# Expert layer with stationary gate and up weights, packed weight transfers, a gather that skips empty rows, and down products of two tiles at a time

## What is computed

```python
x = hidden_states.reshape(-1, 512)                 # 448 tokens
probs = softmax(x @ router_w.T)                    # 32 experts
rw, sel = top_k(probs, 8); rw = rw / sum(rw)
for e in range(32):                                # w_gate, w_up: 512 x 192; w_down: 192 x 512
    w_e = sum(where(sel == e, rw, 0))
    h = silu(x @ wg[e]) * (x @ wu[e])
    acc += (h @ wd[e]) * w_e[:, None]
```

## Time and profile before

| | |
|---|---|
| median of 3 runs | 379.27 us (377.68 to 379.84) |
| profiled execution, its own time | 377.78 us |
| its span, first to last instruction | 375.9 us |
| busy: PE, DVE, ACT, POOL | 84%, 42%, 36%, 42% |
| expert loop, first `gate_up` to the last `down` | 136.5 to 358.5 us |
| moved by DMA | 88.6 MB |

### The profile page before, as it was taken

The page is one execution under the profiler, slowest core; times in us unless marked ns, Lnnn a source line. Parts: engine busy times, 40 slices in busy tenths (PEclk is TensorE's granted clock), DMA queues, the critical chain, the costliest instruction groups (busy, mean ns, idle before and its releaser), DMA issues.

```text
span 375.9 us, 4754 instructions
## 1 busy us (share of the span) xinstructions
PE 313.9 (84%) x1131; PEld 173.2 (46%) x1131; DVE 156.2 (42%) x465; ACT 137.0 (36%) x226; POOL 156.1 (42%) x144
## 2 busy tenths in 40 slices
PE   5799734558869469999999999999999999999910
PEld 1345211235536235555555555555555555555500
DVE  3348798174687833323322332332233233222102
ACT  3245738984873302222322322232232223223200
POOL 5304438643351122454355345435534543553230
PEclk9999976589989559999999999999999999999985
DMA  8599920097048331669999999999999999999667
GB/s 301 205 361 414 373 72 1 0 265 237 3 130 292 117 89 30 112 123 296 311 311 322 329 316 312 323 302 295 305 309 298 300 293 308 293 295 313 128 117 231
DMA packets 31310, 88.63 MB, mean 236 GB/s; under 512 B 4497, under 2 KB 4625, under 8 KB 30529
## 3 DMA queue, kind: packets, MB, share of 16 engines
q1 hardware_dynamic: 21936, 66.38, 51.7%
q0 software_dynamic: 8960, 21.63, 27.3%
q10 hardware_dynamic: 402, 0.48, 0.4%
HBM read 73.46 MB, written 15.02 MB: 235 GB/s over the span
## 4 chain that ended last, share of the span: by engine, by line
PE 66%; DVE 16%; ACT 5%; DMA 5%; issue 4%; POOL 2%; SPq 0%; DVEq 0%; POOLq 0%; ACTq 0%
PE ps L1025 30%; PE ps L1046 18%; PE ps L1035 5%; PE ps L1015 3%; DVE stats L1098 2%; PE ps L1054 2%; PE ps L901 2%; PE ps L851 2%; PE ps L927 2%; DMA sum<-w_t,add_idx 2%; ACT w_t L682 2%; DVE raw L1199 1%; POOL root_out L528 1%; DVE big L1193 1%; DVE amax L1246 1%
## 5 line engine op out<-in xcount | busy, mean ns | idle before, releaser
L599 POOL DMA_INDIRECT big<-token_rows,idx x40 | 39.6, 990 | 116.1 <-DVE idx L1338 98.0
L612 POOL DMA_INDIRECT sum<-w_t,add_idx x40 | 63.1, 1577 | 23.2 <-issue 13.0
L1388 DVE SCALAR_TENSOR_TENSOR w_t<-ps,big,w_t 128x192 f32<-128x192 f32 x40 | 16.7, 417 | 126.6 <-ACT w_t L812 126.6
L812 ACT ACTIVATE w_t<-ps 128x192 f32<-128x192 f32 x40 | 13.2, 331 | 109.9 <-PE ps L1025 109.9
L1025 PE MATMUL ps<-raw,w_t 128*128 128x384 f32 x144 | 51.1, 498 | 0.4 <-issue 0.4
L1025 PE MATMUL ps<-big,w_t 128*128 128x384 f32 x144 | 51.2, 499 | 0.0
L806 ACT ACTIVATE w_t<-ps 128x512 f32<-128x512 f32 x40 | 23.9, 597 | 47.6 <-PE ps L1046 47.6
L528 POOL TENSOR_TENSOR root_out<-root_in,minus_half 112x1 f32<-112x1 f32 x20 | 12.8, 640 | 59.1 <-DVE root_in L1111 59.0
L901 PE MATMUL ps<-w_t,q_t 128*112 128x512 bf16 (+1 forms) x96 | 26.1, 431 | 9.9 <-DVE h L1149 5.9
L1025 PEld LDWEIGHTS ps<-raw,w_t 128*128 128x128 f32 x144 | 25.9, 189 | 18.1 <-issue 3.8
L1025 PEld LDWEIGHTS ps<-big,w_t 128*128 128x128 f32 x144 | 25.9, 189 | 17.9 <-issue 3.6
(11 more groups left out here) (162 smaller groups left out, 397.7 us busy)
## 6 DMA issues: line engine op xcount, KB each, us to landing
big<-in_ffn_w_gate SPq DMA_DIRECT2D x18, 384.0 KB, 5.9
big<-in_ffn_w_up SPq DMA_DIRECT2D x18, 384.0 KB, 9.1
raw<-in_ffn_w_gate SPq DMA_DIRECT2D x18, 384.0 KB, 5.8
raw<-in_ffn_w_up SPq DMA_DIRECT2D x18, 384.0 KB, 7.1
raw<-in_ffn_w_down SPq DMA_DIRECT2D x18, 384.0 KB, 6.8
ring<-in_ffn_w_down SPq DMA_DIRECT2D x13, 384.0 KB, 7.2
big<-in_ffn_w_down SPq DMA_DIRECT2D x9, 384.0 KB, 7.5
big<-in_mlp_w_in SPq DMA_DIRECT2D x2, 1536.0 KB, 10.7
```

The lines of the kernel that those rows point to most:

```text
L599: nc.gpsimd.indirect_dma_start(got[:, s, :], None, rows_dram[:, :], bass.IndirectOffsetOnAxis(ap=idx[:, s:s + 1], axis=0)).then_inc(ld_got ...
L612: nc.gpsimd.indirect_dma_start(acc_dram[n][:, :], bass.IndirectOffsetOnAxis(ap=add_idx[:, s:s + 1], axis=0), y[:, s, :], None, compute_op= ...
```

## The change

- **Stationary weights.** `gate_up` holds blocks of 128 weight columns stationary and moves the 128 slots of x. Its output is h already transposed: gate and up of the first 128 hidden values, and one block in which gate and up of the last 64 stand together. 3 blocks x 4 inputs = 12 matmuls. `transpose_h` and its copy are gone. The gate value now enters as a scale in `y_out`.
- **Packed transfers.** The host lays each expert's gate, up and 128 rows of down into one array (`we_main`, 8 KB per row) and the other 64 rows of down into a second (`we_rest`). Two DMAs per expert instead of three. Eight slots, in four pairs; the two tiles of a pair keep their 64 rows in different halves of the 128 partitions. The unroll is U = 8.
- **Down of two tiles.** On even steps PE does `down` of t-2 and t-1: two matmuls with 128 rows, then two with 64 rows, the first in one row half, the second in the other.
- ACT's `y_out` and POOL's scatters of two tiles follow on odd steps.
- **Skipping gather.** Empty slots get an index beyond `token_rows`, and the gather leaves them out.

```diff
@@ gate_up @@
-                wg = gate_up_of(slot_of(st, 0))
+                wg = slots[st.u][:, 0:WG].rearrange("p (c o) -> p c o", c=DC)
                 pe.wait_ge(xt_ready, st.upto(0))
-                pe.wait_ge(ld_gu[st.u], st.landed(0, 32))
+                pe.wait_ge(ld_we[st.u], st.landed(0, 32))
                 wait(pe, hid_ready, st.upto(-2))
-                dst = bank(st.slot(0, 2))[:, 0:2 * IE].rearrange("p (n i) -> p n i", n=2)
-                for c in range(4):
-                    last = nc.tensor.matmul(dst, x_t[:, st.slot(0, 2), c, :], wg[:, :, c, :], start=c == 0, stop=c == 3)
+                for o in range(0, 3 * P, P):
+                    for c in range(DC):
+                        last = nc.tensor.matmul(bank(st.slot(0, 2))[:, o:o + P], wg[:, c, o:o + P], x_t[:, st.slot(0, 2), c, :],
+                                                start=c == 0, stop=c == DC - 1)
                 last.then_inc(gu_done, 1)
@@ down and transpose_h become down_two @@
-                for c in range(2):
-                    last = nc.tensor.matmul(bank(4 + st.slot(d, 2)), h_t[:, st.slot(d, 2), c, :], wd[:, c, :],
-                                            start=c == 0, stop=c == 1)
-                last.then_inc(y_done, 1)
-
-            def transpose_h(st):
...
+                wait(pe, y_ready, st.upto(d - 1))
+                for n in (d, d + 1):
+                    pe.wait_ge(hid_ready, st.upto(n))
+                    nc.tensor.matmul(bank(4 + st.slot(n, 2)), h_t[:, st.slot(n, HS), 0, :], slots[(st.u + n) % U][:, WG:WCOLS],
+                                     start=True, stop=False)
+                for n in (d, d + 1):
+                    nc.tensor.matmul(bank(4 + st.slot(n, 2)), h_t[rest_rows(st, n), st.slot(n, HS), 1, :],
+                                     slot_rest[(st.u + n) % U], start=False, stop=True).then_inc(y_done, 1)
@@ PE's loop @@
                 place_row(st, 3)
                 gate_up(st)
                 transpose_x(st, 1)
-                down(st, -1)
-                transpose_h(st)
-            down(Step(st.k, U - 1), 0)
+                if st.u % 2 == 0:
+                    down_two(st, -2)
+            down_two(Step(st.k, U - 2), 0)
@@ ACT's loop @@
             for st in steps_from(act, more_i, more_ready):
+                if st.u % 2:
+                    y_out(st, -3)
+                    y_out(st, -2)
                 act.wait_ge(gu_done, st.upto(0))
                 wait(act, hid_ready, st.upto(-1))
-                nc.scalar.activation(sg[:, :], bank(st.slot(0, 2))[:, 0:IE], ACT.Silu).then_inc(silu_ready, 1)
+                nc.scalar.activation(sg[:, 0, :], bank(st.slot(0, 2))[:, 0:P], ACT.Silu)
+                nc.scalar.activation(sg[IB:P, 1, :], bank(st.slot(0, 2))[0:IB, 2 * P:3 * P], ACT.Silu).then_inc(silu_ready, 1)
                 x_turned(st, 1)
-                y_out(st, -1)
@@ DVE's loop @@
+                dve.wait_ge(ld_got[s], st.gathered(0))
+                wait(dve, y_ready, st.upto(-4))
+                nc.vector.tensor_copy(gate_w[:, s:s + 1], gate)
                 dve.wait_ge(silu_ready, st.upto(0))
-                dve.wait_ge(ld_got[s], st.landed(0))
-                wait(dve, ht_done, st.upto(-2))
-                nc.vector.scalar_tensor_tensor(hid[:, st.slot(0, 2), :], bank(st.slot(0, 2))[:, IE:2 * IE], gate, sg[:, :],
-                                               ALU.mult, ALU.mult).then_inc(hid_ready, 1)
+                wait(dve, y_done, st.upto(-HS))
+                nc.vector.tensor_tensor(h_t[:, st.slot(0, HS), 0, :], bank(st.slot(0, 2))[:, P:2 * P], sg[:, 0, :], ALU.mult)
+                nc.vector.tensor_tensor(h_t[rest_rows(st, 0), st.slot(0, HS), 1, :], bank(st.slot(0, 2))[IB:P, 2 * P:3 * P],
+                                        sg[IB:P, 1, :], ALU.mult).then_inc(hid_ready, 1)
                 find(st, 3)
-                dve.wait_ge(ht_done, st.upto(0))
-                wait(dve, y_done, st.upto(-2))
-                nc.vector.tensor_copy(h_t[:, st.slot(0, 2), :, :], bank(6)[0:IH, 0:2 * P].rearrange("p (c t) -> p c t", c=2)
-                                      ).then_inc(ht_ready, 1)
                 keep(st)
@@ POOL's gather and loop @@
-                                             bass.IndirectOffsetOnAxis(ap=idx[:, s:s + 1], axis=0)
-                                             ).then_inc(ld_got[s], 16)
+                                             bass.IndirectOffsetOnAxis(ap=idx[:, s:s + 1], axis=0),
+                                             bounds_check=TOK - 1, oob_is_err=False).then_inc(ld_got[s], 16)
...
                 gather(st, 3)
-                scatter(st, -1)
+                if st.u % 2:
+                    scatter(st, -3)
+                    scatter(st, -2)
+            scatter(Step(st.k, U - 1), -1)
             scatter(Step(st.k, U - 1), 0)
@@ SP's loads @@
-            def load_gate_up(slot, e, u):
-                sp.dma_start(slot[:, 0:WG // 2], we_gate_v[e, :, :]).then_inc(ld_gu[u], 16)
-                sp.dma_start(slot[:, WG // 2:WG], we_up_v[e, :, :]).then_inc(ld_gu[u], 16)
-
-            def load_down(slot, e, u):
-                sp.dma_start(slot[0:IH, WG:WCOLS], we_down_v[e, :, :]).then_inc(ld_dn[u], 16)
...
+            def load_expert(e, u):
+                sp.dma_start(slots[u], we_main[e, :, :]).then_inc(ld_we[u], 16)
+                sp.dma_start(slot_rest[u], we_rest[e, :, :]).then_inc(ld_we[u], 16)
...
-                    sp.wait_ge(gu_done, st.upto(0))
-                    load_gate_up(loop_slot[u], bass.ds(e, 1), u)
                     sp.wait_ge(y_done, st.upto(0))
-                    load_down(first_slot[u] if u == U - 1 else loop_slot[u], bass.ds(e, 1), u)
+                    load_expert(bass.ds(e, 1), u)
```

More of the change, by code:

```diff
@@ L27 @@
 ROWS = P + TOK
-IH = IE // 2
-WG = 2 * 4 * IE
-WCOLS = WG + 2 * D
+IB = IE - P
+WG = 2 * DC * IE
+WCOLS = WG + D
+PAIR = 2 * WCOLS + D
 MAGIC = 1.5 * 2.0 ** 23
@@ L34 @@
 FAR = 1024.0
-U = 4
+NO_TOKEN = 1024
+U = 8
 EPS6, EPS5 = 1e-6, 1e-5
 N_ROOTS = 6 * NG
+HS = 4
 def wait(eng, sem, value):
@@ L82, in steps_from @@
     eng.wait_ge(more_ready, 1)
-    last = eng.value_load(more_i[0:1, 0:1], min_val=0, max_val=7) + (NE // U - 1)
+    last = eng.value_load(more_i[0:1, 0:1], min_val=0, max_val=4) + (NE // U - 1)
     with eng.Fori(1, last) as k:
@@ L113, in program @@
         rows = late(NG * ROW)[0:G, :].rearrange("p (g r) -> p g r", g=NG)
-        got = late(4 * ROW).rearrange("p (s r) -> p s r", s=4)
         mask_pm = late(TOK)[0:NE, :]
+        lent = late(2 * I1)
+        swg = lent[0:G, :].rearrange("p (s i) -> p s i", s=2)
+        got = lent[:, 0:4 * ROW].rearrange("p (s r) -> p s r", s=4)
         assert at[0] <= 11 * D
-        swg = big[0:G, 11 * D:11 * D + 2 * I1].rearrange("p (s i) -> p s i", s=2)
         w_t = sb("w_t", [128, DC * 2 * I1], BF16)
@@ L256, in patch_bank, with rest_rows @@
             return ps[:, b + c // 4, (c % 4) * G:(c % 4 + 1) * G]
[L258 to L274, removed]
+        def rest_rows(st, d):
+            return slice((st.u + d) % 2 * IB, ((st.u + d) % 2 + 1) * IB)
         ld_x = [sem(f"ld_x{g}") for g in range(NG)]
@@ L283, in program @@
         ld_wdown = [sem(f"ld_wdown{n}") for n in range(DC)]
-        ld_gu = [sem(f"ld_gu{n}") for n in range(U)]
-        ld_dn = [sem(f"ld_dn{n}") for n in range(U)]
+        ld_we = [sem(f"ld_we{n}") for n in range(U)]
         ld_got = [sem(f"ld_got{n}") for n in range(4)]
@@ L456, in _ @@
+            sp.wait_ge(t1_done, NG)
+            load_expert(0, 0)
+            load_expert(1, 1)
+            sp.wait_ge(wt_ready, 11)
+            load_expert(2, 2)
+            load_expert(3, 3)
+            sp.wait_ge(wd_ready, DC)
+            load_expert(4, 4)
+            load_expert(5, 5)
             sp.wait_ge(swg_ready, NG)
             sp.wait_ge(ssq2_ready, NG)
-            for t in (5, 6):
-                sp.wait_ge(ld_gu[t % U], 32)
-                sp.wait_ge(ld_dn[t % U], 16)
-                load_expert(t)
@@ L484, in _ @@
                     sp.wait_ge(y_done, st.upto(0))
-                    load_down(first_slot[u] if u == U - 1 else loop_slot[u], bass.ds(e, 1), u)
+                    load_expert(bass.ds(e, 1), u)
+            for u in range(U):
+                st = Step(last - 1, u)
+                e = sp.value_load(owner_row[0:1, bass.ds(st.tile(U), 1)], min_val=0, max_val=NE - 1)
+                sp.wait_ge(y_done, st.upto(0))
+                load_expert(bass.ds(e, 1), u)
             end = Step(last, U - 1)
@@ L1403, in laid_out @@
     import numpy as np
+    blocks = np.concatenate([we_gate[:, :, :P], we_up[:, :, :P], we_gate[:, :, P:], we_up[:, :, P:]], axis=2)
+    main = [blocks.reshape(NE, DC, P, 2 * IE).transpose(0, 2, 1, 3).reshape(NE, P, WG), we_down[:, :P, :]]
     return {
```

116 lines of the change are left out of this document (44 added, 72 removed).

## The result

The kernel after takes 429.75 us in the median (425.93 at the lowest) beside 379.55 us for the kernel before. One of its four runs took 1032.74 us at a granted clock of 1.00, for a reason that isn't known; the ratio, 1.128 with a 95% interval from 1.116 to 1.140, leaves it out, and the median of the other three is 428.8 us. The forecast was 402.6 us with a range of 390 to 422, so the direction was right and the size was not: some 27 us are missing, and the time lies above the range.

The account below looks back on a forecast made before the run. PE's instruction stream was taken to bound the loop. Its steps summed to 236.7 us against 214.67, +22.0; with tail +1.2, 377.78 became 401.0 profiled, 402.6 us as median, range 390 to 422.

Parts of the forecast that it names:

- What bounds the kernel: Expert loop: PE's instruction stream sets the time, busy 44.00 of 44.00 us, one period 5.48 us.
- `gate_up`, transposes, `place_row`: PE's own work per step: 24 weight passes 2.82 us, four transposes of x 0.47, place_row 0.29.
- Down of two tiles: PE, even steps: full passes 1.72 us, half passes 1.29 with only neighbours in different halves overlapping, two mode changes 0.09 each.
- halves wholly paired: Rival, even steps: all half passes overlap, 0.86 us, -8 us, 395 in all; chance 0.12 shared with cheaper passes.
- serial halves: Rival, even steps: half passes never overlap, +0.43 us on 19 pairs, +8, 410 in all; chance 0.21.
- The odd step: PE waits bare for DVE's index after gate_up: 2.99 + 2.11 (2.0 to 2.35) + 0.29 = 5.39 us.
- Scatter in pairs: POOL's scatters and DVE's keep waiting on them: loop of 12.05 us at the median, hidden under the 12.16 us pair.
- L: Time from a scatter's start to its landing: median 8.2 us, at most 9.6, expected smaller after the change.
- Packed transfers, skipped rows, SP's order: DMA: fewer, larger weight transfers, shorter gather and new order before the loop cost and bring nothing, +-1 us at loop start.
- The tail: After the last gate_up: PE ends sooner, but two scatters follow each other; +1.2 us (0 to 3).
- PE isn't held on odd steps: Rival: index ready whenever PE arrives, odd step 3.58 us, 18 save 32.6, 369 in all; chance 0.05.
- The clock falls in the pauses: Rival: PE's clock drops in pauses of 1.6 us, passes per pair about double, some 580 us; chance 0.01.

## Why the prediction was right, and where it failed

**What bounds the kernel** held for the kernel after: PE's stream, with its pauses, sets the loop's time.

**`gate_up`, transposes, `place_row`** held: 24 passes take 2.78 us start to start (269.49 to 272.27) against 2.82; the four transposes 0.43 against 0.47; `place_row` 0.29.

**Down of two tiles** was set too high. Full passes to half passes 1.82 (266.32 to 268.14), half passes to `place_row` 1.06, together 2.88, where 1.72 + 1.29 + 0.09 + 0.09 = 3.19 was forecast. The even step at full clock is 6.38 instead of 6.77 (249.16 to 255.54 in the kernel with the pause filled). The wrong term is the 1.29 for half passes of which only the neighbours A low and B high were to overlap (1.38 with the change behind it, against 1.06). By the rule of the Trainium skill ("TensorE: Matmul & The Clock Gate", Part 3) as the prediction used it, that order gives 1.29; the run says 1.06, and 1.11 for one tile's two. Two passes do run together, as it says, but the trace shows them starting two and two (268.14 x2, above) and not in the order that was assumed. The rival "halves wholly paired" was right in this, and "serial halves" wrong. The even steps give back 0.39 x 17, and the last two, without `place_row`, 0.30 each: 7.2 us.

**The odd step** held in its mechanism: a pause on every odd step, ended by DVE's index, from the same chain as in the earlier trace rows. Its size was 0.22 short, 2.33 us against 2.11, from the end of `gate_up`. The two silus cost 0.59 up to the product against 0.43 in the earlier trace rows, +0.16 where +0.225 was set; the two products, 0.63 up to `find` against 0.33, cost +0.30 where +0.09 was set; from the index to `place_row` it is 0.34 against 0.27. Each of the two products starts 0.31 behind the last operation, so the overlap of 0.08 that I carried over from the single product is not there. `gate_up` itself ends 0.05 sooner than set. The odd step takes 5.56 against 5.39, 0.17 x 18 = 3.1 us.

**Scatter in pairs** held: it was hidden. In the kernel after the landing is 4.6, 5.1 and 5.5 us at least, in the middle and at most in the loop's line, so L was smaller, as set, and `keep` waited for 2.8 us in all:

```profile
DVE add_idx L1319 <- DMA sum<-w_t,add_idx: 2.8, 6, 1.0
```

It became the bound once the pause and the wait for x were gone, which shows that it was next in line. Its price beside L, 3.85 us, wasn't tested in this kernel; the chain without the products took 3.43.

**Packed transfers, skipped rows, SP's order** brought nothing that shows, as set. Only the skipping was tried by itself. The loop began 1.8 us later, but that need not be their cost: the kernel before with the pause added, whose code up to the loop is unchanged, began at 138.18 us, and the kernel after with the products on even steps at 136.76.

**The tail** was set at +1.2 and is +2.5. The last scatter started 10.62 us behind the last `gate_up`'s start, as forecast (10.5):

```profile
401.75 2.94 PE L1004 MATMUL ps<-w_t,raw 128*128 128x128 f32 x24
...
412.37 1.56 POOL L583 DMA_INDIRECT sum<-w_t,add_idx  x1 [1.02 <-issue]
```

The other 1.4 us are behind it, where reading the sums back took 5.82 us against 3.84.

**"PE isn't held on odd steps"** didn't come true, for the reason given. The limit that the prediction named for that case, 4.3 us an odd step and some 382 us with the copy of x as the only wait, is near what the kernel with `find` first shows: 4.21, and 380.28 us. The total agrees by some luck, since the even steps were shorter than in that sum and waits for the scatter came in.

**The clock is the step that failed.** "The clock falls in the pauses" had a chance of 0.01 and a price of 580 us, and both were wrong. So the sum put the clock at nothing, and that was the failed step: the clock did fall, 18 falls x 1.63 = 29.3 us, and 1.6 more in the second step's `gate_up`. With the rest (even steps -7.2, odd steps +3.1, start +1.8, tail +1.3) that makes +29.9, against the 29.7 that were missing. Two readings led past it. The first is the evidence: the earlier trace rows says clock 1.00 with PE busy for half of 102 to 106 us, and I took that as a sign that idling does no harm. The two windows behind it, in the same trace of the kernel before, say otherwise:

```profile
106.00:110.00 4.00, 1.82 (x16) 1.00 (x15) 2.98 (x6) 2.88 (x3) 1.94 (x2) 1.00 0.37 111
110.00:114.00 4.00, 3.64 (x20) 2.05 (x19) 3.13 (x10) 2.37 (x2) 1.33 (x2) 0.57 0.90 299
```

PE is half idle up to 110 us at 1.00, and when it is busy again the clock is at 0.57. The fall comes late, in the stretch behind the idle one, so the clock of an idle window doesn't show whether a fall follows. The second is the price: I doubled all passes of a pair, as if the clock stayed low. It comes back within the next `gate_up`. The right price was one slow `gate_up` per pause, 4.57 - 2.94 = 1.63, and could have been bounded from the first `gate_up` at low clock, 5.07 against 2.69: at most 2.4 a pause, 18 x 2.4 = 43, so 401 to 444 us. With a fair chance for it the range would have held the time.

**What stays open.** Why every long pause of the kernel after is followed by a fall, and about the same pause in two other kernels by few (2 and 6 of 18). Why the loop starts at 136.8 to 140.3 us in kernels with the same code ahead of it. And what holds back the version with eight index slots and the transposes first.

## What to carry to other kernels

Work that is bunched into every second step leaves the other step short, and a chain that was hidden comes out there: compare each step by itself with the longest chain that it must cover, and not their mean. Move the head of that chain (here `find`) before the work is thinned, and then look for the next wait in line, here the index slots of the scatter. And price a pause of TensorE with what follows it: look at the granted clock behind the idle stretches of the trace, not in them.

## What the hardware did that I had not expected

- A pause of 1.82 to 1.90 us in PE's stream was followed by the clock at 0.50 for 3.4 us, beginning 0.2 to 1.7 us after PE had resumed, in every pair of the kernel after; pauses of 1.04 us by none. The same pause of 1.89 us with more work around it was followed by a fall only twice.
- Adding work made a kernel faster: two products of zeros in the pause took 429.75 us to 401.45.
- Four half passes of 512 columns of two tiles, in different row halves of PE, took 1.06 us, and two of one tile 1.11; they start two and two.
- A scatter of 128 rows landed after 5.1 us in the median where the transfers ran at 256 GB/s, and after 8.2 at 318.
- Gather and scatter with skipped rows moved as many packets as without skipping, and no gain in time showed.
